# Projection and experts: four blocks unrolled, the close of each block moved into the next

## The reference, cut to what matters

```python
# end of the attention: attn is [2048, 2048], out_w.T is [2048, 256]
attn = attn * rsqrt(mean(attn**2, -1) + 1e-5) * norm_w
y = (sigmoid(x @ gate_w.T) * attn) @ out_w.T
x = layernorm(x + y)

# experts: 16 routed and 2 shared, hidden width 176 each, top 4 of 16
out = 2 * x + sum_e gate[:, e] * (relu(x @ w1[e] + b1[e]) @ w2[e] + b2[e])
x = layernorm(out)
```

## Time and profile before

| what | value |
|---|---|
| median of 3 runs | 2061.4 us (2059.46 to 2062.37) |
| profiled execution, its own time | 2062.64 us |
| its span, first to last instruction | 2060.8 us |
| mean granted TensorE clock | 0.948 |
| busy, share of span: PE, DVE, ACT, POOL | 86%, 60%, 43%, 23% |
| projection, first matmul to end of last turn | 651.3 to 762.2 us |
| layernorm after it, to the next phase's first load | 764.0 to 779.4 us |
| experts, first matmul to end of last turn | 804.3 to 1108.6 us |

### The profile page before, as it was taken

One profiled execution on the slowest core, in us unless ns is written; L12 is line 12 of the kernel. 1 busy time (PEld: TensorE's weight loads), 2 busy tenths in 40 slices (PEclk: granted clock), 3 DMA queues, 4 the chain that ended last, 5 costly groups with the idle time before them and its releaser, 6 DMA issues. The chain is left out here.

```text
span 2060.8 us, 44154 instructions
## 1 busy us (share of the span) xinstructions
PE 1772.5 (86%) x16556; PEld 1348.5 (65%) x16556; DVE 1240.7 (60%) x3036; ACT 879.8 (43%) x1538; POOL 475.4 (23%) x428
## 2 busy tenths in 40 slices
PE   6999999999998875999996566667889999998886
PEld 5888888888886663777774122223457777777775
DVE  0034443444444564644444889997198888889975
ACT  4533323333333333444443554453255555555652
POOL 1223332334336006800000276663000000000000
PEclk9999999999999986999998788889899999999998
DMA  2000000000003006323321000000322121212111
GB/s 87 18 2 23 23 19 4 23 23 23 11 12 105 0 0 180 91 87 87 93 87 42 0 1 0 0 0 0 117 84 84 44 84 43 85 43 85 49 79 42
DMA packets 55494, 96.82 MB, mean 47 GB/s; under 512 B 11424, under 2 KB 38176, under 8 KB 52776
## 3 DMA queue, kind: packets, MB, share of 16 engines
q1 hardware_dynamic: 55260, 94.95, 14.4%
q10 hardware_dynamic: 108, 0.15, 0.0%
HBM read 92.57 MB, written 2.51 MB: 46 GB/s over the span
## 5 line engine op out<-in xcount | busy, mean ns | idle before, releaser
L1359 POOL TENSOR_TENSOR sc_sb_bx<-sc_sb_dtx,sc_sb_bs 128x1024 f32<-128x1024 f32 x64 | 150.7, 2355 | 84.0 <-DVE sc_sb_h L1371 70.3
L1833 ACT ACTIVATE re_sb_z<-re_ps_misc 128x512 bf16<-128x512 f32 x192 | 105.8, 593 | 136.3 <-PE re_ps_misc L1647 93.5
L1371 DVE TENSOR_TENSOR_SCAN sc_sb_h<-sc_ps_a,sc_sb_bx 128x512 f32<-128x512 f32 x128 | 150.4, 1207 | 20.8 <-ACT sc_ps_a L1349 20.8
L544 POOL TENSOR_TENSOR g_sb_squares_sum<-g_sb_squares_sum,at_sb_qT 128x512 f32<-128x512 f32 x64 | 81.8, 1278 | 310.2 <-ACT at_sb_qT L475 310.2
L1075 DVE TENSOR_TENSOR mo_sb_gated<-mo_sb_hidden,mo_sb_gate 128x512 f32<-128x512 f32 x100 | 72.5, 725 | 131.5 <-ACT mo_sb_hidden L1045 131.0
L1045 ACT ACTIVATE mo_sb_hidden<-mo_ps_h,mo_sb_b 128x512 f32<-128x512 f32 x100 | 68.8, 688 | 162.2 <-PE mo_ps_h L1003 161.9
L1292 PE MATMUL sc_ps_y<-sc_sb_hc,all_sb_ident 128*128 128x512 f32 x256 | 126.8, 627 | 0.0
L1734 PE MATMUL re_ps_out<-re_sb_up,re_sb_W 128*128 128x256 f32 x512 | 121.1, 381 | 0.9 <-ACT re_sb_W L1818 0.9
L506 DVE COPY at_sb_state<-at_ps_state_sum 128x128 f32<-128x128 f32 x64 | 18.6, 290 | 168.9 <-PE at_ps_state_sum L420 168.9
L1734 PEld LDWEIGHTS re_ps_out<-re_sb_up,re_sb_W 128*128 128x128 f32 x512 | 95.7, 190 | 18.6 <-issue 4.5
L515 DVE SCALAR_TENSOR_TENSOR g_sb_gated<-at_ps_out,at_sb_nw,g_sb_gated 128x512 f32 x64 | 48.1, 751 | 94.3 <-ACT at_sb_qT L475 94.3
(11 more groups left out here) (252 smaller groups left out, 4921.5 us busy)
## 6 DMA issues: line engine op xcount, KB each, us to landing
re_sb_b_all<-re_b SPq DMA_DIRECT2D x16, 2048.0 KB, 8.4
mo_sb_gate<-mo_gates SPq DMA_DIRECT2D x36, 256.0 KB, 3.3
mo_sb_w<-in_w_dram SPq DMA_DIRECT2D x10, 640.0 KB, 9.7
at_sb_w<-in_qkv_w_dram SPq DMA_DIRECT2D x18, 256.0 KB, 3.0
mo_sb_gate<-mo_gates SPq DMA_DIRECT2D x20, 192.0 KB, 2.8
mo_sb_gate<-mo_gates SPq DMA_DIRECT2D x16, 224.0 KB, 3.0
at_sb_tbl<-in_decay_dram SPq DMA_DIRECT2D x18, 193.5 KB, 2.3
mo_sb_gate<-mo_gates SPq DMA_DIRECT2D x20, 160.0 KB, 2.7
```

Of the source, the lines that this page charges most:

```text
L544: nc.gpsimd.tensor_tensor(part, part, qT[n][:, :], ALU.add).then_inc(summed, 1)
L1359: nc.gpsimd.tensor_tensor(bx[g % BXS][:, :, :], dtx[:, :, tokens(g)], bs[g % BSS][:, :].unsqueeze(1).broadcast_to([P, KD, BLK]), ALU.mult) ...
L1371: nc.vector.tensor_tensor_scan(h[g % 2][:, d, :], a[g % 2][d][:, :], bx[g % BXS][:, d, :], 0.0, ALU.mult, ALU.add).then_inc(scanned, 1)
L1833: nc.scalar.activation(z[:, n, :, 4 * j:4 * j + 4, :], misc[j % 2][:, :].rearrange("p (r a t) -> p a r t", r=4, a=2), ACT.Copy).then_inc(S ...
```

## The change

Both loops over blocks are written out, so that all buffer numbers and wait values are constants, and the close of a block is moved into the next one:

- Projection: the second pair of accumulators takes two of the four banks that held the sums of squares (`ps_sum[0:2]`), so PE needs no wait to begin a block. The multiplication of block `i - 1` (`scale`) stands on DVE behind tile 2 of block `i`, its transposes on PE behind tile 2, and its addition on DVE behind tile 5 (`FLIP`, `ADD = 2, 5`).
- The addition in the projection now makes the statistics too (4 `bn_stats` per block), and the layernorm behind it makes none.
- Experts: the 100 tiles of all blocks are one list of jobs. PE does rows of job `n`, sums of job `n - 2`, through the block ends. The accumulators are two pairs, for which the hidden rows have two banks instead of three (`NP = 2`). The close of block `i - 1` stands at jobs 3, 5 and 7 of block `i`: ACT's copies (`KEEP`), PE's transposes (`FLIP`), DVE's additions and statistics (`ADD`).
- The last block of each phase closes as before. Nothing is left out of the computation; no load is moved.

```diff
         ps_sum = [s.ps(f"sum{n}") for n in range(NBLK)]
+        bank = [[s.ps(f"bank{n}") for n in range(KD)], ps_sum[0:KD]]
...
-                with pe.Fori(0, NBLK) as i:
-                    pe.wait_ge(scaled, i * KD + KD)
+                for i in range(NBLK):
+                    if i == 1:
+                        pe.wait_ge(rooted, NBLK)
+                    if i >= 2:
+                        pe.wait_ge(scaled, (i - 1) * KD)
+                    to = bank[i % 2]
                     for a in range(PAIRS):
                         pe.wait_ge(wo_low, a + 1)
                         pe.wait_ge(G_low, i * PAIRS + a + 1)
                         for d in range(KD):
                             of = slice(d * P, (d + 1) * P)
-                            nc.tensor.matmul(bank[d][:, :], woH[:, a, of], GH[a % NG][:, :], start=(a == 0), stop=False)
-                            nc.tensor.matmul(bank[d][:, :], woH[:, a, of], GL[a % NG][:, :], start=False, stop=False)
-                            last = nc.tensor.matmul(bank[d][:, :], woL[:, a, of], GH[a % NG][:, :],
+                            nc.tensor.matmul(to[d][:, :], woH[:, a, of], GH[(i * PAIRS + a) % NG][:, :], start=(a == 0), stop=False)
+                            nc.tensor.matmul(to[d][:, :], woH[:, a, of], GL[(i * PAIRS + a) % NG][:, :], start=False, stop=False)
+                            last = nc.tensor.matmul(to[d][:, :], woL[:, a, of], GH[(i * PAIRS + a) % NG][:, :],
                                                     start=False, stop=(a == PAIRS - 1))
                         last.then_inc(used, 1)
-                    res.tensor(pe, i, scaled, i * KD + 2 * KD)
+                        if i and a == FLIP:
+                            res.tensor(pe, i - 1, scaled, i * KD)
+                res.tensor(pe, NBLK - 1, scaled, NBLK * KD)
...
+                def scale(i):
+
+                    dve.wait_ge(inverted, i * 4 + 4)
+                    dve.wait_ge(used, (i + 1) * PAIRS)
+                    for d in range(KD):
+                        nc.vector.tensor_tensor(res.y[:, d, :], bank[i % 2][d][:, :], inv[:, i * BLK:(i + 1) * BLK],
+                                                ALU.mult).then_inc(scaled, 1)
+
...
+                        if i and a == FLIP:
+                            scale(i - 1)
+                        if i and a == ADD:
+                            dve.wait_ge(x_loaded, 16)
+                            res.vector(dve, i - 1)
+                scale(NBLK - 1)
+                res.vector(dve, NBLK - 1)
...
-        NP = 3
+        NP = 2
         ps_h = [s.ps(f"h{n}") for n in range(NP)]
-        acc = [s.ps(f"acc{n}") for n in range(KD)]
+        acc = [[s.ps(f"acc{n}{d}") for d in range(KD)] for n in range(2)]
...
+        JOBS = [(i, f) for i in range(NBLK) for f in range(FTILES)]
+        KEEP, FLIP, ADD = 3, 5, 7
...
+                def rows(n):
+                    i, f = JOBS[n]
+                    fs = slice(f * P, (f + 1) * P)
+                    pe.wait_ge(x_low, i + 1)
+                    pe.wait_ge(w_low, 2 * f + 2)
+                    if n >= NP:
+                        pe.wait_ge(relu_ready, n - NP + 1)
...
+                def sums(n):
+                    i, f = JOBS[n]
+                    if f == 0 and i >= 2:
+                        pe.wait_ge(y_ready, (i - 1) * KD)
+                    pe.wait_ge(low_ready, n + 1)
...
+                for n in range(len(JOBS) + 2):
+                    if n < len(JOBS):
+                        rows(n)
+                    if n >= 2:
+                        sums(n - 2)
+                    if n >= FTILES and n < len(JOBS) and n % FTILES == FLIP:
+                        res.tensor(pe, n // FTILES - 1, y_ready, n // FTILES * KD)
+                res.tensor(pe, NBLK - 1, y_ready, NBLK * KD)
...
+                def keep(i):
+                    act.wait_ge(used, (i + 1) * FTILES)
+                    if i:
+                        act.wait_ge(res.turned, i * KD)
                     for d in range(KD):
-                        nc.scalar.activation(res.y[:, d, :], acc[d][:, :], ACT.Copy).then_inc(y_ready, 1)
+                        nc.scalar.activation(res.y[:, d, :], acc[i % 2][d][:, :], ACT.Copy).then_inc(y_ready, 1)
+
+                for n, (i, f) in enumerate(JOBS):
+                    act.wait_ge(h_product, n + 1)
+                    if n >= 2:
+                        act.wait_ge(gated_ready, n - 1)
+                    nc.scalar.activation(hidden[n % 2][:, :], ps_h[n % NP][:, :], ACT.Relu,
+                                         bias=b1[:, f:f + 1]).then_inc(relu_ready, 1)
+                    if n >= 1:
+                        high(n - 1)
+                    if i and f == KEEP:
+                        keep(i - 1)
+                high(len(JOBS) - 1)
+                keep(NBLK - 1)
...
+                for n, (i, f) in enumerate(JOBS):
+                    dve.wait_ge(relu_ready, n + 1)
+                    dve.wait_ge(gate_loaded[n % NG], loads(n))
+                    if n >= 2:
+                        dve.wait_ge(low_ready, n - 1)
+                    nc.vector.tensor_tensor(gated[n % 2][:, :], hidden[n % 2][:, :], gate[n % NG][:, :],
+                                            ALU.mult).then_inc(gated_ready, 1)
+                    if n >= 1:
+                        low(n - 1)
+                    if i and f == ADD:
+                        res.vector(dve, i - 1)
+                low(len(JOBS) - 1)
+                res.vector(dve, NBLK - 1)
...
-        layernorm_phase(nc, M, stats_ready=False)
+        layernorm_phase(nc, M)
```

More of the change, by code:

```diff
@@ L776, in _ @@
[L776 to L782, removed]
+                        reuse(dve, i, a)
+                        dve.wait_ge(G_high, i * PAIRS + a + 1)
@@ L966, in experts_phase, with loads, block_of @@
         res = Residual(nc, M, s, 2.0)
-        def done(i, f):
-            return i * FTILES + (FTILES + f + 1)
-        def loads(i, f):
-            each = [16 * len(gate_segments(n)) for n in range(f % NG, FTILES, NG)]
-            return i * sum(each) + sum(each[:f // NG + 1])
+        JOBS = [(i, f) for i in range(NBLK) for f in range(FTILES)]
+        KEEP, FLIP, ADD = 3, 5, 7
+        def loads(n):
+            return sum(16 * len(gate_segments(JOBS[m][1])) for m in range(n % NG, n + 1, NG))
+        def block_of(i):
+            return slice(i * BLK, (i + 1) * BLK)
         with nc.Block() as block:
@@ new lines, in rows @@
+                def rows(n):
[5 more added lines that the diff above has]
+                        pe.wait_ge(relu_ready, n - NP + 1)
+                    for c in range(KD):
+                        xs = (slice(None), c, block_of(i))
+                        nc.tensor.matmul(ps_h[n % NP][:, :], w1H[:, c, fs], xH[xs], start=(c == 0), stop=False)
+                        nc.tensor.matmul(ps_h[n % NP][:, :], w1H[:, c, fs], xL[xs], start=False, stop=False)
+                        last = nc.tensor.matmul(ps_h[n % NP][:, :], w1L[:, c, fs], xH[xs],
+                                                start=False, stop=(c == KD - 1))
+                    last.then_inc(h_product, 1)
@@ new lines, in sums @@
+                def sums(n):
[3 more added lines that the diff above has]
+                    pe.wait_ge(low_ready, n + 1)
+                    for d in range(KD):
+                        of = slice(d * P, (d + 1) * P)
+                        to = acc[i % 2][d][:, :]
+                        nc.tensor.matmul(to, w2H[:, f, of], gatedH[n % NH][:, :], start=(f == 0), stop=False)
+                        nc.tensor.matmul(to, w2H[:, f, of], gatedL[n % NH][:, :], start=False, stop=False)
+                        last = nc.tensor.matmul(to, w2L[:, f, of], gatedH[n % NH][:, :],
+                                                start=False, stop=(f == FTILES - 1))
+                    last.then_inc(used, 1)
```

120 lines of the change are left out of this document (32 added, 88 removed).

## The result

The changed kernel took 2027.6 us (median of 4 runs, 2025.8 to 2030.05) against 2061.9 of the kernel before on the same chip: a ratio of 0.984 (0.982 to 0.985). The profiled execution took 2029.0, its span 2027.2; against the profiled 2062.6 that is 33.6.

The account below looks back on a forecast made before the run. PE was taken to bound the kernel (busy 86% of the span), with stops at block ends. Projection 13.8, experts 7.7 and layernorm 3.8 sum to 25.3, so 2061.4 becomes 2036 us; range 2030 to 2044, about 0.85.

Parts of the forecast that it names:

- part 2: Projection, DVE: inserted work delays tile 6's cut; PE stops 0.5 per block end, 1.5 in all (bounds 0 and 4.2 per block).
- part 4: Experts, ACT and DVE: ACT's copies hidden, PE stops 1.2 per block for DVE's low part (bounds 0 and 2.9).
- part 1: Projection, PE: three stops and their low clock go, 18.2 (third stop's clock 0.1); turns of 0.95 stay, 2.9 in all.
- A: Rival, projection: the low clock comes at the new, shorter stops too, so its loss is not won: 2040; chance 0.12.
- B: Rival, projection and experts: DVE's inserted work is not hidden: 2052, halfway there 2044; chance 0.12.
- D: Rival, code: each new instruction block stops PE for 3.0, 27 against 25.3: 2063; chance 0.03, plus 0.02 for a part.
- Rival C: More is won: DVE's new stops don't occur (1.5 + 3.6) and the layernorm gives 4.4: 2030; chance 0.12.
- Part 5: Layernorm behind the projection: finding its statistics saves 5.44, less the last block's statistics: gain 3.8 (bounds 3 and 4.4).
- Part 6: Code: constants save only hidden operations; about nine more instruction blocks cost PE 0 (bounds 0 and 27).

Follow-up runs that it names:

- again: Both kernels timed and profiled once more without an edit: 2062.0 us for the kernel before, 2025.6 us for the changed one, ratio 0.983.
- doubled statistics: Changed kernel with four more statistics per block but the last, in both phases, into a spare tile nobody reads: 2037.0 us, ratio 0.989.
- unrolled: Kernel before with both loops written out with constants, order of work unchanged: 2058.7 us, ratio 0.9987.
- spread: Changed kernel with two statistics each behind two later tiles of the experts: 2026.3 us, ratio 0.983 to the kernel before.
- statistics alone: Kernel before with statistics made at the projection's block ends, and the layernorm that finds them: 2060.7 us, ratio 1.000.
- longer code: 64 tiny unused matmuls ahead of the scan, in both kernels: 2062.4 us in the kernel before, 2026.7 us in the changed one.

## Why the prediction fell short

The measured gain was 34.3 where 25.3 were forecast. Two steps failed. One is what DVE's inserted work costs PE (parts 2 and 4: stops of 1.5 and 3.6 forecast, none and 2.0 measured). The other is the clock behind the third stop of the old projection (in part 1 about 0.1, in four of six profiles some 2.7). Smaller terms add to them, and 2.6 us stay open.

**Direction and main mechanism: right.** PE goes from block to block without a gap in the projection, the low clock behind its block ends is gone, the experts stop where it was said, and no wait for issue came in either phase. Of the rivals, A fell (1.00 across the new block ends, even over the doubled statistics' stops of 1.1), B fell (the burst is covered in the projection), D fell (unrolled gained, and the code in the experts moved 10 blocks, in the projection 4, with no wait). Rival C, "more is won", came nearest, with a chance of 0.12. Its conditions held in part: DVE's stop did not occur in the projection and did, at half, in the experts. The rule of the Trainium skill (Runtime: NRT & Kernel Launch, section Instruction fetch mechanics), which gave 0 for the code, agrees with both phases.

**Part 1, the stops of PE: 18.2 less 2.9.** Right for the profile it was made from: without stops of part 2 it gives 15.3, and 109.8 - 94.2 = 15.6 (94.2 in four profiles of the new projection; the first one shown has 95.4). But its term for the third stop, 0.1, was one profile's chance and is mis-sized: four of six profiles with the old projection have the low clock there too, for some 2.7 more. The old projection takes 109.8 to 113.4 in the profiles of its order of work (statistics alone aside), the new one 93.9 to 95.4.

**Part 2, DVE in the projection: this step failed.** It had DVE's inserted work make PE stop for 0.5 per block end, 1.5 in all; there are no such stops. Three small terms were each too large: the burst takes 2.63 by starts and not 1.28 + 0.24 + 1.40 = 2.92; operations of DVE that stand back to back begin some 0.08 before the former's row ends (676.31 + 0.69 against 676.92), so that sums of durations are too long; and DVE's cut starts 676.31 - 675.58 = 0.73 behind ACT's instead of 0.86, as the register operations in front of its waits are gone (unrolled alone shows the same). Together 0.6 (9.04 instead of 9.65), enough to turn 0.3 late into 0.2 early.

**Part 4, DVE in the experts: the same step, mis-sized.** 1.2 forecast per block, 0.66 measured (0.55 and a slower first matmul; spread wins back 0.66 too). The turn cost 0.88 instead of 0.95 (0.79 to the next matmul, whose interval is 0.09 longer). So a block gave 4.72 - 0.88 - 0.66 = 3.18 instead of 2.57; the three give 9.5 instead of 7.7.

**Part 5, the layernorm: right by its own rows.** From its statistics to the next phase's load it takes 760.45 - 748.81 = 11.64 instead of 15.39: 3.75, forecast 3.8. But the rows were laid too narrowly: in the kernel before, statistics began 764.01 - 761.09 = 2.92 behind the last turn, in the next phase; now they stand in the same one and begin 2.02 behind it. That is 0.9 more.

**Part 6, code and constants: the code right, the constants not.** They were put at nothing as "all hidden". Unrolled alone gained 2.7, 0.43 of it per block of the experts, and part 2 above lost its stop partly by them.

**The router** took 0.7 less; it was not forecast. It goes with the written-out projection: 20.4 to 20.7 from the router's first matmul to the experts' where that stands (unrolled alone has 20.4), 21.1 to 21.3 where the loop stands. What in it does this was not tried.

**Summed up** over three pairs of profiles (both kernels first, again, and with longer code), in us:

| stretch | mean gain | forecast |
| --- | --- | --- |
| projection | 17.0 | 13.8 |
| last turn to the router | 4.8 | 3.8 |
| router | 0.8 | 0 |
| experts | 10.3 | 7.7 |
| together | 32.8 | 25.3 |
| by the medians of the runs (34.3, 36.4, 35.4) | 35.4 | 25.3 |

So of the ten us beyond the forecast, 1.5 are the stops of part 2 that did not come, 1.8 the third stop's clock (2.7 in two of these three profiles), 1.8 the shorter stop and turn of part 4, 1.0 the layernorm, 0.8 the router, and 0.6 other clocks that differ from profile to profile. **The last 2.6 us stay open.** In the profiles nearly all of them lie behind the experts, where nothing was edited. The retrieval takes 599.6 to 607.9 in 14 profiles (mean 606.4 in the six with the old experts, 603.3 in the eight with the new ones), although its instructions are the same. What varies is PE's waits called issue: 15.9 to 22.0 in total, and they go with the length of the phase (correlation 0.79). Length of code did not move the time. Whether the means differ by more than chance, 14 profiles don't tell.

**The range** ended at rival C's 2030 exactly. It left no room below it for what one profile can't show: clocks and issue waits that differ by 2 to 4 us from run to run.

## What to carry to other kernels

Where work is put into the shadow of a bottleneck (where it runs while another engine is the one waited for), lay it out by distances from start to start, not by durations: over ten operations the sum of small overlaps can decide between a stop and none. A cheap experiment, the same work doubled, shows how much cover is left. Work moved off an idle stretch pays only if its new place has cover; the same statistics cost nothing in the new order, where they shortened the layernorm by 3.8, and gained nothing in the old. A low clock behind a stop, or its absence, read in one profile, is chance: price every stop of the same kind with it, and look at a second profile before a few us are put down to a cause.

## What the runs showed of the hardware

- The granted clock behind like stops differs from run to run: behind the projection's third stop 1.00 over 24.1 us in one profile and 0.88 over 27.9 in the next; at the experts' start 0.71 and 0.89.
- Writing a loop out took 0.43 per block of 73.96 off the experts. In the projection DVE's cut then starts 0.74 behind ACT's instead of 0.87. That the 0.43 are won at the block end, where PE waits for such a chain, fits this; it was not tried by itself.
- In the retrieval, dense in short matmuls, PE has waits called issue of 15.9 to 22.0 us in total, differently each time, while ten blocks of code moved in during the experts brought no such wait.
- Rows of DVE that stand back to back begin some 0.08 before the former's row ends: the operation behind one of 0.69 starts 0.61 after it (676.31 and 676.92).
- Fifty-five small matmuls ahead of a phase kept its first 18 matmuls at the full clock in one profile (0.39 instead of 0.63 per row; behind the wait of 2.9 that followed the clock was low again), and did not in another, whose first 14 ran at the low clock. Neither gained.
